# One router round reordered: the logits' transposes ahead of the centring, variances and projection inside the next round

## What is computed

```python
# end of L0 attention, out: the recurrent state's read-out (8, 512, 128)
mu = jnp.mean(out, axis=-1, keepdims=True)
var = jnp.mean((out - mu) ** 2, axis=-1, keepdims=True)
out = (out - mu) / jnp.sqrt(var + LN_EPS) * ln_g + ln_b
x = x + (out * jax.nn.silu(x_in @ Wg)) @ Wout
# L0 router, on xn = layernorm(x)
logits = jax.nn.relu(xn @ rw1 + rb1) @ rw2 + rb2
vals, ids = jax.lax.top_k(logits, 2)
pos = jnp.cumsum(one_hot(ids), axis=0) - 1       # place of a token with its expert
keep = pos < CAP
disp = zeros((E, CAP, C)).at[ids, pos].add(xn * keep)
```

## Time and profile before

| | us |
|---|---|
| median of 3 runs | 928.38 (927.7 to 929.48) |
| the profiled execution | 927.65 |
| its span | 925.6 |

### The profile page before, as it was taken

One profiled execution on the slowest core, in us unless ns is written; L12 is line 12 of the kernel. 1 busy time (PEld: TensorE's weight loads), 2 busy tenths in 40 slices (PEclk: granted clock), 3 DMA queues, 4 the chain that ended last, 5 costly groups with the idle time before them and its releaser, 6 DMA issues.

```text
span 925.6 us, 18384 instructions
## 1 busy us (share of the span) xinstructions
PE 774.7 (84%) x6154; PEld 469.3 (51%) x6154; DVE 693.2 (75%) x2078; ACT 622.2 (67%) x932; POOL 632.3 (68%) x414
## 2 busy tenths in 40 slices
PE   4965765669998689468787989999999999999997
PEld 1343221224543357323233756767776777777775
DVE  7769899985777558498999878776666666666664
ACT  3755233323455367248778988888888888989895
POOL 4008899730577727558798997686868686868695
PEclk9987899899999899879999999999999999999999
DMA  5999300008200030252600000000000000000000
GB/s 150 118 120 202 115 0 0 18 3 211 69 21 7 3 101 26 68 149 58 204 1 1 1 1 2 13 1 11 0 11 0 8 4 0 11 0 11 0 13 13
DMA packets 52761, 40.47 MB, mean 44 GB/s; under 512 B 6028, under 2 KB 44703, under 8 KB 52703
## 3 DMA queue, kind: packets, MB, share of 16 engines
q1 hardware_dynamic: 49630, 37.28, 18.5%
q0 software_dynamic: 3072, 2.51, 0.9%
HBM read 18.07 MB, written 14.88 MB: 36 GB/s over the span
## 4 chain that ended last, share of the span: by engine, by line
POOL 24%; PE 18%; issue 14%; DVE 14%; ACT 6%; DMA 1%; POOLq 0%; DVEq 0%; ACTq 0%; SPq 0%
POOL scratch L725 20%; PE PS L1874 17%; DVE scratch L1635 2%; DVE resid L1537 2%; DVE stats L1375 1%; DVE scratch L1643 1%; POOL disp L635 1%; POOL resid L711 1%; PE PS L1881 1%; ACT scratch L1163 1%; ACT scratch L1159 1%; DVE resid L1388 1%; DVE A L1400 1%; DVE scratch L1378 1%; ACT A L1094 1%
## 5 line engine op out<-in xcount | busy, mean ns | idle before, releaser
L725 POOL TENSOR_TENSOR scratch<-scratch 128x1024 f16<-128x1024 f32 x128 | 273.0, 2135 | 84.5 <-ACT scratch L1163 82.3
L1822 DVE SCALAR_TENSOR_TENSOR resid<-PS,coef,resid 128x128 f32<-128x128 f32 x512 | 144.0, 344 | 108.8 <-PE PS L1874 103.4
L1874 PEld LDWEIGHTS PS<-A,scratch 128*128 128x128 f16 x3456 | 203.4, 98 | 37.9 <-POOL scratch L725 4.9
L1874 PE MATMUL PS<-A,scratch 128*128 128x128 f16 x3456 | 217.1, 219 | 3.9 <-POOL scratch L725 1.6
L1874 PE MATMUL PS<-A 128*128 (+1 forms) x768 | 186.8, 379 | 0.8 <-DVE A L1666 0.2
L1159 ACT ACTIVATE scratch<-PS,cols 128x512 f32<-128x512 f32 x256 | 163.9, 683 | 25.9 <-PE PS L1874 19.0
L1163 ACT ACTIVATE scratch<-scratch 128x1024 f16<-128x1024 f32 x128 | 135.3, 1057 | 5.0
L1874 PE MATMUL PS<-scratch,ident 128*128 128x512 f32 x160 | 89.4, 681 | 51.9 <-DVE scratch L1341 51.9
L594 POOL TENSOR_TENSOR scratch<-A 128x1024 f32<-128x1024 f32 x32 | 76.0, 2384 | 73.2 <-DVE A L1310 56.2
L1874 PEld LDWEIGHTS PS<-A 128*128 128x128 f16 x768 | 70.7, 98 | 66.6 <-issue 0.7
L635 POOL DMA_INDIRECT disp<-A,scratch x64 | 65.5, 1023 | 36.4 <-issue 30.0
(11 more groups left out here) (334 smaller groups left out, 1321.0 us busy)
## 6 DMA issues: line engine op xcount, KB each, us to landing
A<-A SPq DMA_DIRECT2D x22, 256.0 KB, 7.5
y_rows<-zeros SPq DMA_DIRECT2D x8, 512.0 KB, 6.0
A<-y_rows SPq DMA_DIRECT2D x16, 256.0 KB, 3.5
disp<-zeros SPq DMA_DIRECT2D x4, 528.0 KB, 21.6
A<-disp SPq DMA_DIRECT2D x4, 528.0 KB, 6.0
resid<-in_L_attn_x SPq DMA_DIRECT2D x8, 256.0 KB, 4.0
A<-scratch SPq DMA_DIRECT2D x8, 256.0 KB, 6.9
A<-in_L_ffn_ew SPq DMA_DIRECT2D x1, 2048.0 KB, 12.4
```

The costliest lines, as they stand in the source:

```text
L725: pool.tensor_tensor(h_low[n % 4], h_full[n % 2], h_high[n % 4], SUB).then_inc(S("m1_low"), 1)
L1822: last = STT(out=resid[:, g, :], in0=bank(4 + e % 2)[:, t * C:(t + 1) * C], scalar=coef[b % 2][:, t, e:e + 1], in1=resid[:, g, :], op0=MUL ...
L1874: return nc.tensor.matmul(o, l, r, start=start, stop=stop)
```

## The change

On PE, in rounds 1 to 6: `centre(b + 2)` moves from in front of `router_logits_T(b)` to behind `router_logits(b)`. `variance_o` and `project0` of that batch no longer stand around `router_logits(b)`; they stand in the next round, one behind the other, between the counts and the second half of the hidden tiles. In round 1, where they belong to batch 2, both stand together between the halves. On ACT `square_o(b + 2)` moves behind `xT5_copy(b + 1)`, and `deviation_o` goes between the relus of the next round. On DVE `gate_o(b + 2)` moves from in front of `xT5_low(b + 1)` to behind `route(b)`. On POOL the wait for the logits of batch 1, in the scatter of batch 0, stands before t = 3 and no longer before t = 2. No instruction is added and none is left out.

```diff
--- before.py
+++ after.py
@@ -626,9 +626,9 @@
                 pool.wait_ge(S("rows5"), at(b))
                 pool.wait_ge(S("ids5"), at(b))
                 for t in range(NT):
-                    if t == NT // 2 and b + 1 < B:
+                    if t == (NT // 2 if b else NT - 1) and b + 1 < B:
                         pool.wait_ge(S("lg5_mm"), at(b + 1))
-                    elif t == NT // 2:
+                    elif t == NT // 2 and b + 1 == B:
                         pool.wait_ge(s_eb2_mm, 1)
                     for k in range(TOP0):
                         g = b * NT + t
@@ -871,19 +871,16 @@
             for b in range(B):
                 for h in range(HC0):
                     relu5(b, h)
-                    if (b, h) == (1, 1):
-                        deviation_o(2)
+                    if h == 1 and b >= 1 and b + 1 < B:
+                        deviation_o(b + 1)
                 if b + 1 < B:
                     deviation_x5(b + 1)
-                if b and b + 2 < B:
-                    square_o(b + 2)
                 lgT5_copy(b)
                 if b + 1 < B:
                     xT5_copy(b + 1)
-                if b == 0:
-                    square_o(2)
-                elif b + 2 < B:
-                    deviation_o(b + 2)
+                if b + 2 < B:
+                    square_o(b + 2)
+
             def weights0_high(k):
                 hl, w = ((e0_hl1, e0w1), (e0_hl2, e0w2.rearrange("p e i c -> p e (i c)")))[k // 4]
                 two = slice(2 * (k % 4), 2 * (k % 4) + 2)
@@ -1449,13 +1446,13 @@
             for b in range(B):
                 if b + 1 < B:
                     normalise5(b + 1)
-                if b and b + 2 < B:
-                    gate_o(b + 2)
                 if b and b + 1 < B:
                     xT5_low(b + 1)
                 route(b, b % 2)
                 if b == 0:
                     xT5_low(1)
+                if b and b + 2 < B:
+                    gate_o(b + 2)
                 place_picks(b, b % 2)
                 if b == 0:
                     gate_o(2)
@@ -2040,27 +2037,21 @@
             project0(1)
             for b in range(B):
                 router_hidden(b, range(HC0 // 2))
-                if b == 1:
-                    variance_o(2)
-                elif b:
+                if b >= 2:
                     count_picks(b - 1, (b - 1) % 2)
+                if b >= 1 and b + 1 < B:
+                    variance_o(b + 1)
+                    project0(b + 1)
                 router_hidden(b, range(HC0 // 2, HC0))
-                if b == 1:
-                    project0(2)
-                if b and b + 2 < B:
-                    centre(b + 2)
                 router_logits_T(b)
                 if b + 1 < B:
                     transpose5(b + 1)
-                if b and b + 2 < B:
-                    variance_o(b + 2)
                 router_logits(b)
+                if b + 2 < B:
+                    centre(b + 2)
                 if b == 0:
-                    centre(2)
                     unread(3, 4)
                     count_picks(0, 0)
-                elif b + 2 < B:
-                    project0(b + 2)
             count_picks(B - 1, 1)
             pe.wait_ge(S("o_std"), at(B - 1))
             pe.wait_ge(S("slots"), at(B - 1))
```

## The result

| | before | changed |
|---|---|---|
| median, us | 928.93 (927.7 to 929.64, 4 runs) | 937.2 (936.64 to 939.09, 4 runs) |
| ratio to before | | 1.0098 (1.0084 to 1.0112) |
| profiled execution, us | 927.65 | 936.64 |
| its span, us | 925.6 | 934.6 |
| first to last logits (L2027, now L2024), us | 229.49 to 304.85: 75.36 | 229.42 to 312.38: 82.96 |

The changed kernel is slower by 0.98%. The ratio on the 928.38 us of before is 937.5, with 936.2 to 938.8 as its interval. The forecast was 934.9, its own range 933.5 to 937.0, the wider one 931.5 to 937.5. The sign was right and the size fell short: 937.5 lies above the own range and at the edge of the wider one, and half of the interval lies above both.

The account below looks back on a forecast made before the run. PE and the chain over DVE bound the rounds, POOL close behind. Rounds of 11.92 against 10.51 us start POOL's last scatters 6.52 later: 927.65 becomes 934.2, the median, 0.73 higher, 934.9; own range 933.5 to 937.0, wider 931.5 to 937.5.

Parts of the forecast that it names:

- What bounds the kernel before: Router rounds of 10.51 us: PE and the chain over DVE end within 0.2 us of each other, POOL close behind.
- The round, 11.92 us: PE, transposes to transposes: seven distances sum to 11.92 us against 10.51, 1.41 more in each of five rounds.
- The reason given with it: Matmuls with `w_r`: moving the centring takes the free filler from the relus' wait of 0.84 us, replacing it with nothing.
- the other reading: Same 1.41 us a round: variances, logits and projection leave the shadow of `route`, the centring that of the relus.
- DVE: Counts to normalised rows: with the gate in front, DVE ends 11.04 us after the transposes, 0.9 before the next ones.
- POOL's edit worth nothing, POOL waits in each round: Two scatters issued early in batch 0 gain nothing, as POOL has 10.2 us of work in rounds of 11.9.
- POOL's start of the last twelve, 6.52 us later: After the last logits at 312.39, POOL goes on at 313.17 instead of 306.65 us.
- The twelve scatters as before: End of the stage: the last twelve scatters follow as before, since DVE's splitting of weights moves along with them.
- a way to end lower: Last scatters: if DVE's splitting of weights did not move along, three issues would be shorter, 2.5 us in all.
- Everything behind the stage moves along unchanged: Stages after the router: nothing added to the sum beyond the 6.52 us on the profiled 927.65, giving 934.2.
- a sign of being wrong: Whole kernel: the prediction is wrong if, among other signs, the difference lies outside 230 to 325 us.
- The granted clock: Rival, in the rounds: idle time lowers PE's clock to 0.77, 3.1 us more a round, 950 us; 3%.

Follow-up runs that it names:

- both behind the second half: Changed kernel with variances and projection moved behind the second half of the hidden tiles, in front of the matmuls with `w_r`: ratio 1.0085, median 937.28 us.
- unread in two rounds: Kernel before with seven products that nobody reads added behind the logits of rounds 1 and 2: ratio 1.003, median 930.3 us.
- POOL's waits late: Kernel before with POOL's wait for logits in front of the last token tile in every batch but the last: ratio 1.003.
- once more: Repeats without an edit: the kernel before run again, ratio 0.9994, and the changed kernel run again, ratio 1.0099.
- variances first: Changed kernel with the variances in front of the counts and only the projection behind them: ratio 1.0058, median 933.49 us.
- both smaller doses: Kernel before with seven unread products in rounds 1 and 2 (ratio 1.003), and with them in rounds 1 to 4 (ratio 1.0064).
- centring back: Changed kernel with the centring put back in front of the matmuls with `w_r` in rounds 1 to 5: ratio 1.0103, median 937.38 us.
- POOL's wait back: Changed kernel with POOL's wait of batch 0 back in front of t = 2: ratio 1.01, median 938.68 us.
- unread in five rounds: Kernel before with seven unread products behind the logits of rounds 1 to 5, stretching them to 12.0 us: ratio 1.011, median 938.87 us.

## Why the prediction was right or wrong, point by point

**What bounds the kernel before:** right. The longer chain went straight into the time.

**The round, 11.92 us:** measured 12.00 in all five. Transposes to first half 2.08 (2.07 forecast), to the counts 2.02 (1.95), counts 0.21 (0.27), variances 0.89 (0.75), projection 0.98 (0.99), second half to `w_r` 2.29 (2.29), then 3.53 (3.60). The variances were the term most mis-sized, and by a wrong reading: I began their distance at 263.16, the modelled end of the transposes, where their own row starts at 262.99. From start to start rows 2 give 263.87 - 262.99 = 0.88. That the sum came out within 0.08 is in part luck: terms too small by 0.22 and terms too large by 0.14 met. Five rounds: 0.4 us.

**The reason given with it:** half wrong. I wrote that the centring taken from the relus' shadow is the step that the new order loses. The run with the centring put back showed no gain, so that sentence was false, although the sum beside it was right: it was made along the chain. I had also written the other reading, in which variances and projection lose the shadow of `route`, and that one holds. They were beside `route` on DVE; now 1.87 us of them stand between the counts and the second half, where `route` has just ended.

**DVE:** right that it is not the bound; its rows end 1.30 us ahead, not 0.9. I had counted from the counts, and the trace and the run with both behind the second half show that DVE's part starts from the projection.

**POOL's edit worth nothing, POOL waits in each round:** right for the edit. The wait is 1.9 to 2.2 us in five rounds, against 1.5 to 2 forecast, and missing in the last one.

**POOL's start of the last twelve, 6.52 us later:** measured 7.02. Of the 0.50 more 0.40 are the rounds, and 0.10 is POOL, which is held by its own eight scatters and not by the last logits.

**The twelve scatters as before:** wrong by 0.54 us. More of them met DVE's splitting of weights, which came 7.71 us later (322.76 against 315.05) where the scatters came 7.02 later. I had named that as a way to end lower; it went the other way. Up to the last scatter 7.56 us are lost, with 6.52 forecast.

**Everything behind the stage moves along unchanged:** this step failed most, by 1.44 of the 2.5 us that the sum fell short of the profiled execution (936.64 against 934.2). I put the stages behind 325 us at nothing, without a reason, in the sum and in its ends, and named a difference there as a sign of being wrong; that sign came. The granted clock was among the rivals, but for the rounds, where it stayed at 1.00 in the changed kernel. Behind the stage it fell to its lower level in stretches of the experts' first matmuls (0.63 us) and of the second attention (466 to 486 us, 1.20 us), where two profiles of before have none of it; 0.39 us came back elsewhere. That the low clock costs this time is shown by the rows. Why it falls there once the stage is shifted stays open.

**The range** was made of the terms' ends in the stage and took in nothing for the stages behind it. Those moved by 0.6 to 2.7 us in ten profiles with a shifted stage (602.99 to 604.69 against 602.02 and 602.36), so its upper end had to be some 2 us higher.

## What to carry to other kernels

To price a reordering in a loop across engines, follow the closed chain from one round to the next and add the distances on it. An idle piece that loses its filler costs nothing if the time opens somewhere else on the same chain; what costs is a product placed between two steps of the chain that used to touch. Rows of an odd round of the same loop, here the last one, give such distances ready made. And what a shift of a stage does to the stages behind it has to stand in the range.

## What the runs showed of the hardware

The granted clock of TensorE differs from kernel to kernel on instructions that no edit touched. The experts' first matmuls, and the second attention from about 406 us on, ran at 2.4 GHz in both profiles of before. In the second attention all ten profiles with a shifted stage have stretches at 1.2 GHz: one costs 1.15 us (unread in two rounds), two cost 1.1 to 1.2 (seven profiles), three cost 2.3 and 2.4 (old order with POOL's waits late, both behind the second half).

All profiles spend 17 to 20.5 us at the lower level around the fetch of the experts' outputs, where PE stands idle for some 16 us. A further stretch came 18 to 20 us after the last logits, while PE ran unread products (before, once more, variances first, both smaller doses), or 25 to 27 us after them, on the experts' first matmuls, where it cost 0.6 to 1.4 us (changed, once more, centring back, POOL's wait back), or not at all (unread in five rounds, POOL's waits late, both behind the second half). The old order with five stretched rounds and the changed kernel had their last scatter at 330.75 and 330.80, and only the second had it. That speaks against the position in time as the only cause, but it is one profile against four. Whether the idle pieces of PE in the new rounds have a part in it is not shown: two kernels with the new order and such pieces, variances first and both behind the second half, lose nothing in the experts. I have not settled what decides.

A short copy or cast on VectorE can be held until an indirect scatter of GpSimd ends, and it depends on where in the scatter it starts. Over all twelve profiles the `CAST` and `COPY` of `route` that start 0.55 to 0.79 us behind the start of a scatter of 0.97 us end together with it and take 0.18 to 0.42 us. Those that start 0.16 to 0.26 us behind it take 0.17 us (45 of them, against 80).
